# A two-layer graph network on one core: in the edge pass, work of GpSimd and TensorE handed to ScalarE and to a mask, new orders on all engines, GpSimd's indirect DMAs in pairs

## The reference

```python
h = jnp.maximum(_layernorm(x), 0.0)
m = concat([h[dst], h[src]]) @ W_pre.T + b_pre          # one message per edge
mx, mn, s1, s2, deg = segment max, min, sum, sum of squares, count of m by dst
mean = s1 / max(deg, 1);  std = sqrt(relu(s2 / max(deg, 1) - mean * mean) + 1e-5)
agg = concat([mx, mn, mean, std]);  log_deg = log(max(deg, 1) + 1)
scaled = concat([agg, agg * log_deg, agg / log_deg])
x = x + (concat([h, scaled]) @ W_post.T + b_post) @ W_lin.T + b_lin

h = jnp.maximum(_layernorm(x), 0.0)
a = segment sum of edge_attr by dst / max(count, 1)
x = x + relu(concat([h, a]) @ W1 + b1) @ W2 + b2
```

## Time and profile before

| | |
|---|---|
| median of 3 runs | 1627.22 us |
| profiled execution | 1626.46 us, its span 1624.7 us |
| mean granted clock of TensorE | 0.973 of full |
| busy in the span | PE 92%, PEld 77%, DVE 86%, ACT 58%, POOL 76% |
| set-up | 0 to 41 us |
| node pass | 41 to 545 us, PE busy 498.27 us |
| change-over | 545 to 600 us, PE busy 31.25 us |
| edge pass, from 641 to 1605 us | PE busy 913.70 us of 964 |

### The profile page before, as it was taken

How to read it: one execution, slowest core, us unless ns; L and a number is a source line. 1 busy time by engine, 2 the same in 40 slices (tenths; PEclk the granted TensorE clock), 3 DMA queues, 4 the chain that set the end, 5 groups by cost and what they waited for, 6 DMA issues and landing times.

```text
span 1624.7 us, 33700 instructions
## 1 busy us (share of the span) xinstructions
PE 1494.9 (92%) x8747; PEld 1257.4 (77%) x8747; DVE 1397.1 (86%) x4327; ACT 939.8 (58%) x1976; POOL 1236.0 (76%) x1376
## 2 busy tenths in 40 slices
PE   2899999999999759999999999999998999999995
PEld 2799998889999648888777787777777777777783
DVE  5899999999999468899888997988887888888892
ACT  1799999999999534455444453434444444444341
POOL 1778777777778777888888888888888888888833
PEclk9899999999999979999999999999999999999997
DMA  3455555555555622233233333333332323333200
GB/s 88 163 209 206 207 207 201 201 201 204 204 203 206 187 87 85 84 86 90 90 91 92 93 92 91 92 91 89 93 91 79 95 86 89 94 93 93 89 18 15
DMA packets 158898, 197.95 MB, mean 122 GB/s; under 512 B 18912, under 2 KB 115321, under 8 KB 158858
## 3 DMA queue, kind: packets, MB, share of 16 engines
q1 hardware_dynamic: 136906, 149.93, 28.3%
q0 software_dynamic: 21952, 47.55, 9.5%
HBM read 111.11 MB, written 90.17 MB: 124 GB/s over the span
## 4 chain that ended last, share of the span: by engine, by line
PE 82%; DVE 6%; issue 5%; ACT 3%; another core or an unknown queue 3%; DMA 1%; SPq 1%; POOL 0%; DVEq 0%; ACTq 0%; POOLq 0%
PE bank L572 12%; PE bank L621 6%; PE bank L581 6%; PE bank L614 5%; PE bank L691 5%; PE bank L618 5%; PE bank L615 5%; PE bank L624 5%; PE bank L704 5%; PE bank L670 3%; PE bank L593 3%; PE bank L591 3%; PE bank L592 3%; PE bank L555 3%
## 5 line engine op out<-in xcount | busy, mean ns | idle before, releaser
L444 POOL DMA_INDIRECT rows<-table,idx x196 | 208.3, 1063 | 59.7 <-issue 59.7
L450 POOL DMA_INDIRECT y<-nout,oidx x196 | 200.0, 1020 | 70.6 <-issue 70.3
L444 POOL DMA_INDIRECT hs<-table,idx x196 | 204.8, 1045 | 44.7 <-issue 31.2
L614 PE MATMUL bank<-comb_lo,agg_hi 128*128 128x384 f32 x588 | 212.4, 361 | 16.6 <-DVE nout L1019 10.7
L572 PE MATMUL bank<-w_sb,nut 128*128 128x128 f32 x1568 | 202.9, 283 | 5.5 <-issue 4.7
L379 POOL TENSOR_TENSOR runs<-nx,b_all 128x512 f32<-128x512 f32 x98 | 125.9, 1284 | 107.9 <-DVE nx L1029 107.8
L572 PEld LDWEIGHTS bank<-w_sb,nut 128*128 128x128 f32 x1568 | 184.5, 193 | 23.1 <-issue 14.2
L618 PE MATMUL bank<-comb_hi,agg_lo 128*128 128x384 f32 x588 | 200.1, 340 | 0.0
L615 PE MATMUL bank<-comb_hi,agg_hi 128*128 128x384 f32 x588 | 199.5, 339 | 0.0
L781 ACT ACTIVATE nh<-nx,nms,nrs 128x128 f32<-128x128 f32 x392 | 161.8, 484 | 1.1 <-DVE nms L1002 0.5
L621 PE MATMUL bank<-comb_sd,agg_sd 128*128 128x384 f32 x392 | 159.6, 489 | 0.0
(11 more groups left out here) (180 smaller groups left out, 4196.9 us busy)
## 6 DMA issues: line engine op xcount, KB each, us to landing
table<-rows SPq DMA_DIRECT2D x98, 512.0 KB, 2.7
rows<-in_x SPq DMA_DIRECT2D x98, 256.0 KB, 3.1
y<-nout SPq DMA_DIRECT2D x98, 256.0 KB
inv<-inv_row SPq DMA_DIRECT2D x49, 256.0 KB
attr<-in_edge_attr SPq DMA_DIRECT2D x48, 256.0 KB
keep<-keep_row SPq DMA_DIRECT2D x49, 128.0 KB
reset<-reset_row SPq DMA_DIRECT2D x49, 128.0 KB
lift<-lift_row SPq DMA_DIRECT2D x49, 128.0 KB
```

What stands on the lines that cost most here:

```text
L444: pool.indirect_dma_start(out=to[:, s, j, :], out_offset=None, in_=of, in_offset=bass.IndirectOffsetOnAxis(ap=idx[:, s, which, j:j + 1], a ...
L450: pool.indirect_dma_start(out=out, out_offset=bass.IndirectOffsetOnAxis(ap=oidx[:, c % 4, j:j + 1], axis=0), in_=eout[:, c % 2, j, :], in_ ...
L614: pe.matmul(acc[:, 0:SCALERS * P], hi, w_lo, start=(a == MX), stop=False, skip_group_check=True)
```

## The change

Only the set-up and the edge pass change. In the edge pass:

- **GpSimd** loses both 512-wide operations (`xdc`, `attr_mean`). Gathers run 3 chunks ahead, not 4. Indirect DMAs go in pairs, with a one-column addition (`pause`) between two pairs. Its wait is for the same operation one step back.
- The constant of `xdc` and the part of b_pre that passes through layer 0 become `acc_seed`, 384 columns, which **ScalarE** copies into bank 5 or 6 before each tile (`seed`). Layer 0's first matmul accumulates onto it. `mix` then adds the gathered receiver rows themselves.
- The division of the attribute sum goes in front of the sum: ScalarE scales each row of `edge_attr` by 1/count (`scale_attr`, four operations), and the scan takes a mask `keepm` of 32-bit numbers, (count-1)/count, in place of `keep`. SyncE loads this fifth mask row.
- ScalarE copies b2 into bank 7 (`out_bias`) in place of TensorE's matmul.
- b_pre is left out of the messages; `message` is gone, and the messages stay in bank 3 or 4 by turns, where the scans read them.
- The second norm's sum comes from `mix`'s last operation (`accum_out`), the squares from ScalarE (`squares`, four operations with `accum_out`) in place of `moments`.
- All `edge_step` orders are new, and a function `open_sums` runs two matmuls before the first layer-0 tile.

The core of the diff:

```diff
@@ gpsimd
-            def receiver_const(c, i):
...
-                pool.tensor_tensor(xdc[:, c % 2], xd[:, c % 4], edge_const[:], ALU.add).then_inc(sem("e_xdc"), 1)
-            def mean_attr(c, i):
...
-                pool.tensor_tensor(attr_mean[:, c % 2, :], run_attr[:, c % 2, :], inv[:, c % 4, :],
-                                   ALU.mult).then_inc(sem("e_attr_mean"), 1)
...
+            def pause(n, c, i):
+                if c >= 1:
+                    pool.wait_ge(sem(f"e_paused{n}"), c + EU * i)
+                pool.tensor_tensor(pause_go[:, n:n + 1], eps_col[:], eps_col[:], ALU.add).then_inc(sem(f"e_paused{n}"), 1)
...
+                if edge(k + 3):
+                    gather_rows_of(k + 3, i)
+                    pool.wait_ge(sem("e_idx"), k + 4 + EU * i)
+                    go(0)
+                    gather(k + 3, (0, 1), i)
+                if edge(k + 2):
+                    copy_factors(k + 2, i)
@@ tensor
+                pe.wait_ge(sem("e_seeded"), TILES * c + j + 1 + TILES * EU * i)
...
-                    pe.matmul(acc[:, 0:SCALERS * P], hi, w_lo, start=(a == MX), stop=False, skip_group_check=True)
+                    pe.matmul(acc[:, 0:SCALERS * P], hi, w_lo, start=False, stop=False, skip_group_check=True)
...
-                pe.matmul(bank[7][:], ones[:], b2_rows[:], start=True, stop=False, skip_group_check=True)
+                pe.wait_ge(sem("e_b2"), c + 1 + EU * i)
@@ scalar
+            def seed(c, j, i):
+                if c == 0 and j < 2:
+                    act.wait_ge(sem("e_sums_open"), 1)
+                elif j >= 2:
+                    act.wait_ge(sem("e_mixed"), TILES * c + j - 1 + TILES * EU * i)
+                else:
+                    act.wait_ge(sem("e_mixed"), TILES * (c - 1) + j + 3 + TILES * EU * i)
+                act.activation(bank[5 + j % 2][:, 0:SCALERS * P], acc_seed[:], ACT.Copy).then_inc(sem("e_seeded"), 1)
...
+                for j in range(TILES):
+                    last = act.activation(off2[:, j, :], x1[:, b, j, :], ACT.Square, bias=neg2[:, b, j:j + 1],
+                                          accum_out=sq2[:, b, j:j + 1])
@@ vector
-                dve.tensor_tensor(x1[:, c % 2, j, :], acc[:, 0:P], part2[:, j % 2, :], ALU.add).then_inc(sem("e_mixed"), 1)
+                dve.scalar_tensor_tensor(x1[:, c % 2, j, :], acc[:, 0:P], 1.0, part2[:, j % 2, :], ALU.mult, ALU.add,
+                                         accum_out=sum2[:, c % 2, j:j + 1]).then_inc(sem("e_mixed"), 1)
...
+                if have:
+                    scan_attr(k, i)
                 if edge(k - 2):
                     outputs(k - 2, i)
...
-                    scan_max(k + 1, i)
+                    scan_sum(k + 1, i)
                     scan_min(k + 1, i)
-                    scan_sum(k + 1, i)
                     message_mean(k + 1, i)
-                    receiver_low(k + 1, i)
```

337 lines of the change are left out of this document (182 added, 155 removed).

## The result

The changed kernel takes 1519.66 us (median of four runs, 1519.18 to 1520.14). The kernel before, on the same chip, took 1628.54. The ratio is 0.933, with a 95% interval of 0.9315 to 0.9348. The prediction said 1551, with a range of 1538 to 1590. The direction was right, and so was the mechanism of the steady part. The gain was 109 us where 76 were forecast, since the step of the edge pass came out shorter and the change-over from the node pass to the edge pass went the other way.

What follows compares the result with a forecast made beforehand. The prediction took GpSimd to bound the edge pass after a dozen steps, and TensorE after the change. 1626.46 - 82.4 (steady part) + 2.0 (set-up) + 5.0 (change-over) = 1551.1 us, range 1538 to 1590.

Steps and rivals of the forecast that it cites:

- the second regime: Edge pass from 844.8 us, kernel before: GpSimd, its lead used up, sets steps of 21.03 us against 19.28 earlier.
- GpSimd's step of 18.5 us after the change: Edge pass: GpSimd's step becomes 20.7 - 2.6 + 0.4 = 18.5 us, bounds 18.1 and 19.4.
- rival A: Edge pass: GpSimd stays the bound, steps of 19.4 to 20 us, 1576 and up to 1603 us; chance 14%.
- The pause, 0.12 us in the sum: Edge pass, GpSimd: each added one-column addition costs 0.12 us, between nothing and 0.42; three make 0.4 per step.
- TensorE's new step, 18.85 us: Edge pass after the change: TensorE is the slowest at 18.85 us per step, ends 18.7 and 19.2.
- 0.42 us per step: Edge pass, TensorE: dropping the bias matmul saves 0.42 us, from its start to the next matmul's start.
- the four steps behind 19.28: Edge pass, kernel before, 706.0 to 783.1 us: TensorE busy without a gap, 77.1 / 4 = 19.28 us per step.
- The set-up, +2.0 us: Before the node pass: a reciprocal of some 1.3 us and `acc_seed`'s two operations, about 0.65, add 2.0 us.
- The change-over, +5 us with 0 and 10 as ends: Node to edge pass: later gathers and moved work, formerly hidden in an idle stretch, add 5 us.
- The part on the order of the gathers: Node to edge pass: chunk 0's gathers, issued after the last node addition and not before, come some 3 us later.
- The seeds: Edge pass: ScalarE's copies before each tile, 0.55 us each, are covered; cover gone, up to 0.5 us per step.
- VectorE isn't the bound: Edge pass: VectorE is busy some 17 us of a step, with over 1.5 us of slack.

Runs made afterwards that it cites:

- the kernel with early gathers: The changed kernel with chunk 0's eight gathers in front of GpSimd's last node addition, not behind it: 1514.30 us; 1515.69 us on another occasion.

## Why the prediction was right or wrong

- **GpSimd sets the second regime of the kernel before: right.** Shown from both sides: without its division the regime is gone (step 19.32, and 18.54 without the bias matmul as well), with two additions given to the changed kernel it is back from about 861 us on, and a shorter TensorE step alone leaves the mean at 20.76. The last three come from profiles without late semaphores, so the stops are not what makes the regime.
- **GpSimd's step of 18.5 us after the change: too high, and read wrongly.** It follows at 17.86 us. The sum of its rows can't be more or less than the step while it never waits; its slack stands for the most part in small instructions held by VectorE's scans. The prediction counted `go` at its 0.34 us mean as work; unhindered it is 0.19. The sentence on what would refute it, "GpSimd without a wait (A)", was a false test: GpSimd has no wait to speak of, and rival A is still wrong.
- **The pause, 0.12 us in the sum: not visible, since GpSimd isn't the bound.** 1518.71 us without the three.
- **TensorE's new step, 18.85 us: the first step that failed.** The mechanism was right, TensorE busy throughout and its clock 1.00. The size was off by 0.29. The term "0.42 us per step" for the bias matmul is 0.62. The other 0.1 is in the base: the four steps behind 19.28 hold 0.1 more than the 19.18 that the changed kernel takes with the matmul back. One of the four has a wait in the hidden layer, 0.67 us from 717.37 to 718.04 for two matmuls that take 0.46 in the other three and in the changed kernel; that is 0.05 of the mean, and the rest isn't shown. The new orders themselves gave nothing: with the old ones the step is 18.54. With 18.56 in the forecast's own sum, the steady part would be 95.4 and not 82.4 us less.
- **The set-up, +2.0 us: about right.** VectorE's first addition of the node pass started at 44.5 to 46.1 us in the seven profiles of kernels made from the one before, 45.3 on average, and at 46.6 to 48.5 in the eight made from the changed one with the reciprocal in place, 47.6 on average, 2.3 more. In the pair of profiles that the sum is about it is 3.1, and 3.5 at the last node addition.
- **The change-over, +5 us with 0 and 10 as ends: the second step that failed, in sign, and the larger one.** From the last node addition to the fourth step the kernel before takes 85.6 us and the changed one 72.0, 13.6 less. The prediction added what was moved there. It took the kernel before's own change-over as sound, and did not ask why TensorE was busy in it for only 31.25 of 55 us. What stood there are the stops: the three kernels made from the one before that have none take 71.3 to 72.6 us, level with the changed one, and against them the moved work would be near the 0 end. Why the kernel before has the stops in its profiles stays open, so it isn't shown that the change as such removes them. The part on the order of the gathers was right in sign: issued behind the addition they cost 3 to 5 us, which the changed kernel pays.
- **The seeds: right.** ScalarE waits 28.6 us in 41 places in front of a seed. TensorE's matmuls never stand idle for one; its weight loads do for 0.24 us per step at most (9.6 us in 40 places, 641 to 1400 us). A seed takes 490 ns, forecast 550. ScalarE is busy for 13.6 us of a step, forecast 15.6.
- **VectorE isn't the bound: right, with more room than forecast.** It is busy for 15.7 us of a step, forecast 17. `mean_b` is at 667 ns, and the four readings of the accumulator are instructions of their own, 83 ns each:

```profile
L1276 DVE TENSOR_TENSOR mean_b<-runs,inv 128x512 f32<-128x512 f32 x41 | 27.4, 667 | 0.0
L1163 DVE DVE_READ_ACCUMULATOR nx<-bank,part 128x1 f32 x164 | 13.6, 83 | 0.0
```

- **The sum.** Forecast 1551.1; with 18.56 for the step it is 1538.1, and with 13.6 less instead of 5 more at the change-over 1519.5. That this meets the 1519.66 measured so closely is in part luck, since the set-up and the node pass cost 3.5 and not 2.0 and the tail gave 0.9: with all four, 1626.46 - 95.4 - 13.6 + 3.5 - 0.9 = 1520.1, against 1520.14 for the profiled execution. It is an account of two profiles and no test of a cause.

## What to carry to other kernels

An engine that never waits is not thereby the bound: look whether its instructions, the smallest above all, are longer than they are elsewhere, and take the shortest of each form for its floor. A matmul's price is the whole stretch from the neighbour before to the neighbour after, with and without it. When TensorE is starved, its clock may fall behind the gaps, so taking 1.3 us off the engine that starves it can give back more (2.2 us per step here, once the bias matmul was gone), and a second, cheaper edit that TensorE could not use before is then worth its full price. And two kernels whose profiles come from different chips differ by the chips as well: profile the unchanged kernel beside the changed one.

## What the runs showed of the hardware that was not expected

- In the changed kernel a small copy of GpSimd that falls into VectorE's scan over SBUF operands (L1267) ends 21 to 26 ns before the scan does, in 41 steps of 41, and so GpSimd keeps step with VectorE without a semaphore.
- TensorE's semaphores can move up to 10 us after its rows say that the work is done; only the waits of others ("remote") tell it. Five profiles of 18 have it, among them all four of one chip. One kernel had it in 45 steps of 49 there, 1746 us, and not at all on another chip, 1514 us. Its cause is open.
- An indirect DMA of GpSimd takes 0.94 to 1.66 us of the engine (0.97 in the median of the changed kernel) and an idle of 0.14 to 0.31 in front of it; an operation between two of them takes over about half of that idle (0.15 left in front of the gather behind a pause at 548.24 us in the kernel with early gathers).
